# GpSimd's column additions of rows seven and six placed one row later, row seven's behind the first root

## The reference, cut to what matters

```python
def reference(x, adj, W, router_w, w1, b1, w2, b2):
    H = layernorm(x)
    HW = einsum('bnf,fo->bno', H, W)
    A = relu((adj + adj.T) * 0.5)
    D = sum(A, axis=1)
    d = where(D > 0, D ** -0.5, 0)
    L = eye(N) - d[:, None] * A * d[None, :]
    x = x + relu(einsum('nm,bmo->bno', L, HW))
    t = layernorm(x)                       # 16384 tokens of 128
    probs = softmax(t @ router_w.T)        # the best two of 8 experts, their weights scaled to sum 1
    y = t
    for e in range(8):
        y = y + gate[:, e] * (gelu(t @ w1[e] + b1[e]) @ w2[e] + b2[e])
    return x + y
```

## Time and profile before

| what | value |
|---|---|
| median of 3 runs | 878.51 us (876.08 to 878.63) |
| the profiled execution | 875.2 us, its span 873.5 us |
| TensorE products busy | 838.3 us, 96% of the span |
| TensorE weight loads busy | 697.9 us, 80% |
| VectorE busy | 638.9 us, 73% |
| ScalarE busy | 475.8 us, 54% |
| GpSimd busy | 325.1 us, 37% |
| mean granted clock of TensorE | 0.995 of full speed |

### The profile page before, as it was taken

The page is one execution under the profiler, slowest core; times in us unless marked ns, Lnnn a source line. Parts: engine busy times, 40 slices in busy tenths (PEclk is TensorE's granted clock), DMA queues, the critical chain, the costliest instruction groups (busy, mean ns, idle before and its releaser), DMA issues.

```text
span 873.5 us, 14324 instructions
## 1 busy us (share of the span) xinstructions
PE 838.3 (96%) x4098; PEld 697.9 (80%) x4098; DVE 638.9 (73%) x1553; ACT 475.8 (54%) x871; POOL 325.1 (37%) x318
## 2 busy tenths in 40 slices
PE   3678999999999999999999999999999999999998
PEld 3676788888888888888888777888888888888886
DVE  2678645479898644443515599999999999999997
ACT  2696523324243211021110488888888888888886
POOL 1793164474757445555445539101000000000000
PEclk9999999999999999999999999999999999999999
DMA  9991667677765257977778866777877777778872
GB/s 277 327 304 59 241 265 275 242 256 259 256 236 184 85 193 283 325 275 269 254 278 319 307 246 220 281 275 298 296 264 260 262 277 276 278 284 293 291 268 76
DMA packets 93472, 223.00 MB, mean 255 GB/s; under 512 B 8904, under 2 KB 60128, under 8 KB 81520
## 3 DMA queue, kind: packets, MB, share of 16 engines
q1 hardware_dynamic: 88304, 213.23, 69.1%
q0 software_dynamic: 2608, 8.33, 2.4%
q10 hardware_dynamic: 2512, 0.86, 0.4%
HBM read 157.89 MB, written 64.49 MB: 255 GB/s over the span
## 4 chain that ended last, share of the span: by engine, by line
PE 90%; ACT 3%; DVE 3%; POOL 2%; issue 1%; DMA 1%; ACTq 0%; DVEq 0%; POOLq 0%
PE bank L989 13%; PE bank L991 13%; PE bank L990 13%; PE bank L1489 6%; PE bank L1486 6%; PE bank L1473 6%; PE bank L1475 6%; PE bank L1474 6%; PE bank L1487 6%; PE bank L344 3%; PE bank L936 2%; POOL col_sum L604 2%; PE bank L1495 2%; PE bank L474 1%; PE bank L325 1%
## 5 line engine op out<-in xcount | busy, mean ns | idle before, releaser
L1531 ACT ACTIVATE act_h<-bank,b_sb 128x512 f32<-128x512 f32 x256 | 176.3, 689 | 46.7 <-PE bank L1475 42.1
L1573 DVE TENSOR_TENSOR gated<-c_all,act_h 128x512 f32<-128x512 f32 x256 | 177.6, 694 | 25.3 <-ACT act_h L1531 20.3
L1578 DVE TENSOR_TENSOR g_lo<-gated,g_hi 128x512 fp32r<-128x512 f32 x256 | 175.5, 685 | 0.2
L1538 ACT ACTIVATE g_hi<-gated 128x512 fp32r<-128x512 f32 x256 | 159.4, 623 | 5.6 <-DVE gated L1573 5.6
L1449 POOL DMA_DIRECT2D out<-fin x31 | 23.6, 762 | 307.9 <-DVE fin L1586 307.9
L1105 POOL TENSOR_SCALAR z<-x,mv,rstd 128x128 f32<-128x128 f32 x128 | 107.0, 849 | 3.4
L989 PE MATMUL bank<-y_hi,stage 128*128 128x512 f32 x256 | 105.7, 413 | 2.3 <-DVE y_lo L767 2.3
L1051 ACT ACTIVATE z_hl<-bank 128x512 fp32r<-128x512 f32 x32 | 19.1, 597 | 155.2 <-PE bank L936 155.2
L1473 PE MATMUL bank<-z_e,w_hi 128*128 128x512 f32 x256 | 102.8, 402 | 0.1
L1489 PE MATMUL bank<-g_lo,w_hi 128*128 128x512 f32 x256 | 101.0, 395 | 0.8 <-DVE g_lo L1578 0.7
L989 PE MATMUL bank<-y,stage 128*128 128x512 f32 x256 | 101.3, 396 | 0.0
(11 more groups left out here) (133 smaller groups left out, 1487.1 us busy)
## 6 DMA issues: line engine op xcount, KB each, us to landing
c_all<-c_scratch SPq DMA_DIRECT2D x64, 1024.0 KB, 7.8
s_scratch<-stage SPq DMA_DIRECT2D x14, 2048.0 KB, 8.4
stage<-s_scratch SPq DMA_DIRECT2D x14, 2048.0 KB, 7.9
z_e<-z_scratch SPq DMA_DIRECT2D x32, 512.0 KB, 7.0
z_scratch<-z_hl SPq DMA_DIRECT2D x31, 512.0 KB, 2.7
x_raw<-in_x SPq DMA_DIRECT2D x32, 256.0 KB, 6.2
x_res<-in_x SPq DMA_DIRECT2D x32, 256.0 KB, 7.0
r_e<-res_scratch SPq DMA_DIRECT2D x32, 256.0 KB, 2.7
```

The lines of the kernel that those rows point to most:

```text
L1531: act.activation(v.act_h[e % R][:, :], ps_h[e % 2][:, :], ACT.Gelu, bias=v.b1_sb[:, e:e + 1]).then_inc(gelu_done, 1)
L1538: act.activation(v.g_hi[e % R][:, :], v.gated[e % R][:, :], ACT.Copy).then_inc(hi_done, 1)
L1573: dve.tensor_tensor(out=v.gated[e % R][:, :], in0=v.c_all[s][:, e, :], in1=v.act_h[e % R][:, :], op=ALU.mult).then_inc(gated_done, 1)
L1578: dve.tensor_tensor(out=v.g_lo[e % R][:, :], in0=v.gated[e % R][:, :], in1=v.g_hi[e % R][:, :].bitcast(FP32), op=ALU.subtract).then_inc(lo ...
```

## The change

It alters two lines of GpSimd's part of the setup and nothing else. Rows 14 to 8 are added where they were. Row seven's addition moves from step 8 to step 9, where it comes behind `root(0)` and behind the `pr.invert` of job 13. Row six's moves from step 9 to step 10, behind the `pr.invert` of job 14. The name `LAST` (6) is no longer used. VectorE, TensorE, ScalarE and SP keep their order.

```diff
@@ -620,8 +620,10 @@
                 root(0)
             if r >= 4 and jobs(r):
                 pr.invert(pool, jobs(r))
-            if LAST <= j <= MB - 2:
+            if 8 <= j <= MB - 2:
                 add_columns(j)
+            if r in (9, 10):
+                add_columns(j + 1)
         root(1)
```

## The result

| | before | changed |
|---|---|---|
| median | 876.77 us (875.94 to 878.63, 11 runs) | 879.91 us (877.07 to 881.88, 11 runs) |
| profiled execution | 875.2 us, span 873.5 | 877.07 us, span 875.3 |

The ratio of changed to before is 1.0034, 95% interval [1.0021, 1.0047]: 3.0 us slower (1.8 to 4.1). A second series of the same two kernels (e9) gave 879.90 us against 876.84, 1.0041 [1.0026, 1.0055]. The ratio is the record's own estimate and not the quotient of the two medians; in e9 the medians alone differ by 3.1 us.

A forecast was written before the change was run, and what follows sets the result against it. TensorE's products were taken to fill nearly all of the span, so only a delay of the graph stage's first product counts. Median 878.5 + 1.0 us for VectorE's later addition of row five = 879.5 us, range 876.4 to 882.0.

The forecast's parts named there:

- The forecast of no difference beyond 0.3%: Whole kernel: chances of faster 0.07, same 0.77, slower 0.16, with 0.3% being 2.6 us.
- Step (a): VectorE's deg_none before the first root: no addition running, so 0.17 us and the root 1.21 us sooner.
- Step (b): GpSimd from the root on: row six's addition ends at 72.89 instead of 71.08, 1.81 us later.
- Step (c): VectorE's addition of row five waits about 1.6 us for row six, starts 1.0 us later and delays the first product.
- Step (d): TensorE's sums of columns 6 and 5 stall 1.1 and about 1.9 us, costing nothing more if the clock holds.
- Step (e): After the first product: nothing absorbs the delay; sum + 1.0 us, bounds 0 to 2.0.
- The clock: TensorE's half clock on the first nine products costs 1.8 us; left as it is in the forecast, with two rivals.
- The first rival: TensorE's clock falls already in the new hole, slowing passes before the first product: + 2.8 us, 881.3; chance 0.15.
- the sign that the prediction named: TensorE's transposes near 74 us at 0.22 us a piece, listed as showing the forecast wrong.
- The second rival: TensorE's clock is whole for the first products, 1.8 us come back: - 0.8 us, 877.7; chance 0.14.
- The third rival: GpSimd's last x_rstd shuts out VectorE's addition of row five: + 2.0 us, 880.5; chance 0.08.

The follow-up runs named there:

- e9: Changed kernel again, unchanged, beside e10 on the same chip; 879.90 us against 876.84 for before, ratio 1.0041 [1.0026, 1.0055].
- e12: Kernel before with two more pow operations on GpSimd ahead of row seven's addition, to force the collision with deg_none; ratio 1.0026 [1.0009, 1.0043].
- e5: Kernel before, unchanged, profiled for a second trace; single time 878.20 us.
- e6: Changed kernel with TensorE's sums of columns 6 and 5 moved behind the first eight blocks of unit 0; 880.36 us, ratio 1.0046 [1.0031, 1.0062].
- e7: As e6, with VectorE's addition of row five also moved behind the second y_low; 877.22 us, ratio 1.0004 [0.9992, 1.0016].
- e1: Changed kernel with 18, 14 and 10 spare transposes filling most of TensorE's holes; ratio 1.0031 [1.0018, 1.0044].
- e10: The same kernel as e1, run a second time beside the changed kernel; ratio 1.0043 [1.0026, 1.0060].
- e2: Kernel before with 9 spare transposes ahead of the sum of column 6 and 11 ahead of the first product; ratio 0.9994 [0.9981, 1.0006].

## Why the prediction was right or wrong

The time forecast, 879.5 us, is near the measured 879.91 by luck: two errors cancel. The base was 878.5 where 11 runs give 876.77, and the change was + 1.0 where 3.0 was measured. The forecast of no difference beyond 0.3% is neither borne out nor refuted: the measured ratio stands just beyond it, with an interval that reaches to both sides.

- **Step (a), the gain of 1.21 us, failed.** It took the 1.37 us of deg_none in one profiled execution for a property of the kernel. The mechanism was right (e12). But in the other four traces that keep this order row seven's addition ends 0.1 to 0.4 us ahead of deg_none, which then isn't held. The root starts 2.29 us behind the statistics in either order (e5, changed kernel), so the change gives no gain there.
- **Step (b), the sum on GpSimd, was right row by row and wrong in its start.** From root to the end of row six it said 7.42 us (65.47 to 72.89); the trace of the changed kernel has 72.12 - 64.72 = 7.40. Against the first trace row six comes 9.69 - 7.88 = 1.81 us later, as forecast; against the second, which has no stall, 9.69 - 6.70 = 2.99: row seven's addition and one x_rstd. The 0.31 us of idle time that the prediction names there plays no part in its sum, which is 0.98 + 2.04 - 1.21.
- **Step (c), VectorE's wait, was the right place.** Forecast 1.6 us of waiting and 1.0 of delay; measured 2.14, and 9.80 - 8.76 = 1.04 against the first trace, 9.80 - 7.57 = 2.23 against the second. e6 and e7 show that the loss goes with this wait and not with TensorE's. The slack of 0.88 us read in the first trace is there in the second too (0.87). The waiting was put too low because the step let row four's loads hold VectorE: the add was to come 0.6 us sooner of the root's 1.21. It came 1.19 sooner, 67.78 - 62.43 = 5.35 behind the statistics instead of 69.74 - 63.20 = 6.54.
- **Step (d)** put TensorE's stalls at 1.1 and 1.9 us; they are 2.39 and 1.87. By themselves they cost nothing on top, as forecast for a clock that holds: in e1 and e10 the column sums wait for the same counts, the clock is whole, and the first product is 2.3 us late, by VectorE's delay alone. What they cost goes through the clock, which falls in the second of them.
- **Step (e)**, that nothing later takes the delay up, is right to the end of the graph stage: from the first product to the experts it is 415.8 and 415.9 us in the changed kernel, 415.8 in e1 and e10, 416.2 and 416.0 in before. In the experts it doesn't hold in general: the store of `out` makes VectorE wait for 0.24 to 1.62 us, different from trace to trace, and in e1 and e10 it takes back what the setup gained.
- **The clock.** The first rival (the fall comes in the new hole, 0.15) is what both traces of the changed kernel show, with the sign that the prediction named: the projection and the last transposes at twice their time. It put the price at 1.8 us on top of the 1.0; filling the holes brings the first product 1.5 sooner. Its total, + 2.8, is nearer the measured 3.0 than the forecast's + 1.0. The second rival's gain of 1.8 from faster products was wrong: the y_low operations pace those products (e2).
- **The third rival**, row five's addition shut out by the last x_rstd, is refuted: the addition starts at 72.23, 0.14 us behind x_rstd, and takes 0.83 us as ever. By the rule on two SBUF inputs of the Trainium skill (SBUF, State Buffer; Who interferes with whom) it should have been held for the rest of that operation; the trace doesn't agree for this pair. Its rule on tensor_scalar agrees with 1.37 and 1.38 us.

What remains: VectorE's wait is shown as the cause, for the loss goes when it goes (e7), and the traces size its delay at 2.2 us. Of the measured 3.0 us (1.8 to 4.1) and 3.6 us (2.3 to 4.8) the first interval holds 2.2 and the second just doesn't, nor do those of e6 and e10. In the traces of the changed kernel the half clock on the last transposes makes up the rest: 2.2 and 1.4 give the 3.6 us at the experts' start. The times of e1 and e10 don't show the clock's part come back, and in their traces a store takes it; how much of the measured loss is the clock's is open.

## What to carry to other kernels

A stall in one profiled execution is a guess about the others: before a change is built on it, ask which two arrivals have to meet for it, how far apart they are, and look at a second trace. A gain early in a kernel has to be followed to the end: here 1.5 us reached the experts and was lost there to the wait for a store. A helper engine that waits for a result has a free place ahead of it; work put behind the wait instead delays everybody who needs that work, by its own length plus what is queued between. Find the reader of each moved result and its slack (here 0.87 us against a delay of 2.99), and if the reader can't be moved, leave the work where it is.

## What the runs showed of the hardware

- A VectorE tensor_scalar on 128x8 (float32, both sides in SBUF) that starts while GpSimd adds two SBUF tiles doesn't end before that addition does: 1.37 and 1.38 us against 0.17. The operations just ahead of it (deg_row, deg_raw with one PSUM input) were not held.
- Two-input VectorE operations beside a GpSimd pow weren't held (0.83 us for row five's addition in either order). The other way round, the last x_rstd took 1.53 us instead of 1.01 when that addition had begun first.
- TensorE's clock was halved in the second of two holes, of 2.39 and 1.87 us with 0.9 us of work between, and with the holes filled it stayed whole. The half clock put the first product 1.5 us later; on the first products themselves it cost nothing (column sums at 23.77 against 23.69).
- Among executions of one kernel a lower mean granted clock went with a longer time in e12 (0.991 to 0.994: 880.3 us and more; 0.996 and 0.998: 878.8 and less). In the filled kernels e1 and e2 no such tie is seen.
- VectorE's wait in the experts for a 256 KB store to land was 0.24 to 1.62 us in 14 traces, and 0.24 and 0.67 in two traces of one kernel.
